# An attention and expert kernel on one Trainium2 core: the opening stage rebuilt, with folds of four head pairs side by side, five shared PSUM banks, stacks of eight heads moved one by one, and another order of steps

## What is computed

```
q = (xn @ q_a[h]) @ q_b[h];  k = (xn @ k_a[h]) @ k_b[h]     # 16 heads, 256 -> 64 -> 16
v = xn @ v_w.T + v_b
att = softmax(causal(q @ k.T / 4));  y = att @ v
out1 = y @ o_w.T + o_b
probs = softmax(xn @ choice_w.T)        # 8 experts, each takes its 128 best tokens of a batch
out2[tokens of e] += gate * (silu(xn[tokens] @ w1[e]) @ w2[e])
result = x + out1 + out2
```

## Time and profile before

| | us |
|---|---|
| median of three runs | 1244.37 (1242.15 to 1245.09) |
| the profiled execution | 1248.95 |
| its span, first to last instruction | 1247.2 |
| TensorE busy | 1163.1 (93%) |
| VectorE busy | 1013.3 (81%) |
| ScalarE busy | 682.7 (55%) |
| GpSimd busy | 702.6 (56%) |
| mean granted TensorE clock | 0.973 of full |

### The profile page before, as it was taken

One profiled execution on the slowest core, in us unless ns is written; L12 is line 12 of the kernel. 1 busy time (PEld: TensorE's weight loads), 2 busy tenths in 40 slices (PEclk: granted clock), 3 DMA queues, 4 the chain that ended last, 5 costly groups with the idle time before them and its releaser, 6 DMA issues. The chain is left out here.

```text
span 1247.2 us, 26009 instructions
## 1 busy us (share of the span) xinstructions
PE 1163.1 (93%) x8508; PEld 812.9 (65%) x8508; DVE 1013.3 (81%) x3396; ACT 682.7 (55%) x1330; POOL 702.6 (56%) x1021
## 2 busy tenths in 40 slices
PE   6789999999999999999999998869999999999994
PEld 5535556556556555555555554448989999999994
DVE  3589988988889999999999988679967676777762
ACT  2347777777677676676676666543423243333330
POOL 1235354354354354354354366754888888888875
PEclk9779999999999999999999999889999999999997
DMA  7552553553453552552551644224666666566654
GB/s 146 119 120 71 135 121 88 135 120 94 129 120 91 133 120 79 130 134 66 140 132 58 149 113 131 65 72 115 127 126 120 113 125 136 112 114 141 107 77 46
DMA packets 112730, 139.39 MB, mean 112 GB/s; under 512 B 21836, under 2 KB 79828, under 8 KB 112596
## 3 DMA queue, kind: packets, MB, share of 16 engines
q1 hardware_dynamic: 82756, 102.84, 32.3%
q0 software_dynamic: 24576, 33.57, 16.2%
q10 hardware_dynamic: 5264, 1.32, 0.6%
HBM read 53.22 MB, written 33.55 MB: 70 GB/s over the span
## 5 line engine op out<-in xcount | busy, mean ns | idle before, releaser
L808 DVE CUSTOM_DVE_ANT_0 junk<-bank,rowmask 128x256 bf16<-128x256 f32 (+3 forms) x1024 | 446.7, 482 | 48.9 <-PE bank L958 44.9
L660 ACT ACTIVATE probs<-bank 128x512 f32<-128x512 f32 x640 | 365.9, 596 | 134.1 <-PE bank L979 127.3
L560 POOL TENSOR_SCALAR_AFFINE_SELECT probs<-probs 128x256 f32<-128x256 f32 (+1 forms) x640 | 229.3, 372 | 255.7 <-ACT probs L660 252.4
L958 PE MATMUL bank<-kstk,qstk 96*128 96x256 bf16 (+3 forms) x1024 | 249.6, 305 | 14.0 <-DMA kstk<-qk_part 7.7
L979 PE MATMUL bank<-qstk,kstk 98*128 98x256 bf16 (+3 forms) x1024 | 250.0, 306 | 11.8 <-DMA qstk<-maxrow 9.7
L1142 POOL DMA_INDIRECT out_rows<-mixed,rows x128 | 212.1, 1657 | 58.3 <-issue 37.5
L1000 PE MATMUL bank<-probs,vaug 128*32 128x512 f32 (+3 forms) x2048 | 179.7, 446 | 5.0 <-POOL probs L560 5.0
L979 PEld LDWEIGHTS bank<-qstk,kstk 98*128 98x128 bf16 x1024 | 76.3, 98 | 148.3 <-ACT probs L660 91.7
L1166 ACT ACTIVATE hid<-bank 128x512 f32<-128x512 f32 x128 | 76.4, 598 | 172.3 <-PE bank L1259 146.6
L1277 PE MATMUL bank<-w_hi,hid_hi 128*128 128x256 f32 x512 | 147.3, 288 | 0.0
L1277 PE MATMUL bank<-w_hi,hid_lo 128*128 128x256 f32 x512 | 144.9, 283 | 0.0
(11 more groups left out here) (149 smaller groups left out, 2171.7 us busy)
## 6 DMA issues: line engine op xcount, KB each, us to landing
qstk<-qk_part SPq DMA_DIRECT2D x96, 256.0 KB, 5.1
kstk<-qk_part SPq DMA_DIRECT2D x96, 256.0 KB, 5.0
qstk<-in_L_ffn_w SPq DMA_DIRECT2D x32, 512.0 KB
xln<-in_L_attn_hidden_states SPq DMA_DIRECT2D x16, 512.0 KB, 6.7
xn_rows<-xn SPq DMA_DIRECT2D x16, 512.0 KB, 2.9
xres<-in_L_attn_hidden_states SPq DMA_DIRECT2D x16, 512.0 KB, 4.0
out_rows<-xres SPq DMA_DIRECT2D x16, 512.0 KB
out_rows<-mixed,rows POOLq DMA_INDIRECT x128
```

Source lines behind the costliest of these rows:

```text
L560: nc.gpsimd.affine_select(out=block, in_=block, compare_op=ALU.is_ge, fill=0.0, base=0, pattern=[[0, len(cols)], [1, P]], channel_multipli ...
L660: nc.scalar.activation(probs[n % 2][:, 512 * k:512 * k + 512], SCORET[k % 2][:], ACT.Exp, scale=SCALE).then_inc(exp_done, 1)
L808: last = nc.vector.tensor_tensor_reduce(out=junk[k % 2][:, col:col + width], in0=SCORE[score_bank(UN * n + k)][:, col:col + width], in1=ro ...
L958: last = nc.tensor.matmul(SCORE[score_bank(UN * n + k)][:, col:col + width], qstk[b % 2][0:KS, GH * g + h, P * i:P * i + P], kstk[b % 2][0 ...
```

## The change

It touches the opening stage, and with the stacks also every later batch:

- A fold is made in two steps. The new step `foldm` puts the second factor on the stationary side and the transposed first factor on the moving side (128 columns); four pairs of heads write to four strips of 32 partitions. Its result is copied out by ScalarE, and `fold` is now two 128x128 transposes. The columns come out so that a projection tile holds eight neighbouring heads.
- In the opening the shared steps take five banks in turn (two shared, two of `scoret`, one of the values' product); from the first `score` on, two in turn as before.
- Each projection tile is stacked as soon as it is ready: four times six DMAs per batch, of half the size. In batch 0 the six of k's first eight heads are issued by ScalarE's queue (new step `stack`), and the first scores wait for the first eight heads of q and of k alone.
- The loads are in another order (one of q_a first, then x, then the rest; the other weights are issued by ScalarE only ahead of `fold` 1), and so are the steps. The projections of batch 1 begin after eight units of scores instead of after one; the transposes of its xn stand among the scores.
- 42 transposes of the identity into a bank that nobody reads (`warm`).
- The bias products move behind the first scores.

```diff
-    out = [("xload", 0, 0), ("lnstat", 0, 0), ("lnstat", 0, 1), ("lnapply", 0, 0), ("xload", 1, 0)]
-
-    out += foldt(0) + [("fold", 0, 0)] + foldt(1) + [("xt", 0, 0), ("xt", 0, 1), ("fold", 1, 0)]
-    out += foldt(2) + qk(0, 0) + foldt(3) + qk(0, 1)
-    out += [("mid", 0, 0), ("fold", 2, 0), ("mid", 0, 1), ("fold", 3, 0), ("wv", 0, 0), ("wv", 1, 0)]
-    out += [("lnstat", 1, 0), ("lnstat", 1, 1)] + qk(0, 2) + qk(0, 3)
-    out += [("mid", 0, 2), ("v", 0, 0), ("mid", 0, 3), ("v", 0, 1), ("v", 0, 2), ("lnapply", 1, 0), ("v", 0, 3)]
-    out += [("xt", 1, dt) for dt in range(DT)] + [("wo", dt, 0) for dt in range(DT)] + [("ob", 0, 0)]
+    out = [("warm", 16, 0), ("xload", 0, 0)] + foldt(0) + [("lnstat", 0, 0), ("lnstat", 0, 1)]
+
+    out += [("foldm", 0, 0), ("fold", 0, 0), ("warm", 8, 0)] + foldt(1) + [("lnapply", 0, 0), ("xload", 1, 0), ("warm", 8, 0)]
+    out += foldt(2) + [("foldm", 1, 0), ("xt", 0, 0), ("xt", 0, 1), ("fold", 1, 0)] + foldt(3) + [("foldm", 2, 0), ("fold", 2, 0)]
+    out += [("qk_first", 0, 0), ("foldm", 3, 0), ("qk", 0, 0), ("fold", 3, 0), ("mid", 0, 0), ("qk_first", 0, 2), ("qk_first", 0, 1)]
+    out += [("qk", 0, 2), ("qk", 0, 1), ("mid", 0, 2)] + qk(0, 3) + [("wv", 0, 0), ("wv", 1, 0), ("warm", 10, 0)]
+    out += [("stack", 0, 2), ("mid", 0, 1), ("mid", 0, 3), ("lnstat", 1, 0), ("lnstat", 1, 1), ("v", 0, 0), ("v", 0, 1)]
+    out += [("wo", 0, 0), ("wo", 1, 0), ("v", 0, 2), ("v", 0, 3), ("lnapply", 1, 0)]
     for t in range(UN):
         out.append(("score", 0, t))
-        if t in (0, 2, 4, 6):
-            out += qk(1, t // 2)
-        if t in (2, 4, 6):
-            out.append(("mid", 1, t // 2 - 1))
+        out += {2: [("xt", 1, 0)], 4: [("xt", 1, 1)], 6: [("bias", 0, 0)], 7: qk(1, 0), 9: qk(1, 1)}.get(t, [])
     for t in range(UN):
-        out += [("score", 1, t)] + [("maxt", 0, 0)] * (t == 2) + [("maxd", 0, 0)] * (t == 3) + [("mid", 1, 3)] * (t == 4)
+        out += [("score", 1, t)] + [("maxt", 0, 0)] * (t == 2) + [("maxd", 0, 0)] * (t == 3)
+        out += {1: [("mid", 1, 0)] + qk(1, 2), 4: [("mid", 1, 1)] + qk(1, 3), 6: [("mid", 1, 2)], 8: [("mid", 1, 3)]}.get(t, [])
     for t in range(UN):
         out += [("scoret", 0, t), ("score", 2, t)] + [("maxt", 1, 0)] * (t == 3) + [("maxd", 1, 0)] * (t == 4)
+        out += [("ob", 0, 0)] * (t == 5)
...
+    for n, s in enumerate(shared):
+        bank_at[s] = n % 5 if n < len(opening) else n % 2
...
-            SCORE, SCORET, Y, SHARED = banks[0:3], banks[3:5], banks[5], banks[6:8]
+            SCORE, SCORET, Y, SHARED = banks[0:3], banks[3:5], banks[5], banks[6:8] + banks[3:6]
...
-                        elif kind == "mid" and k % 2 == 1:
-
-                            if n >= 2 and k == 1:
+                        elif kind == "mid":
+
+                            if n >= 2 and k == 0:
                                 sp.wait_ge(scoret_ready, at(UN * GB * (n - 1), 8 * UN))
                                 sp.sem_inc(sp_past, 1)
-                            sp.wait_ge(lo_done, at(GB * n + k + 1, 2 * GB))
-                            side = k // 2
+                            sp.wait_ge(lo_done, at(GB * n + turn(n, k) + 1, 2 * GB))
+                            side, m = divmod(k, 2)
                             stk = (qstk, kstk)[side][n % 2]
+                            landed = first_heads if n == 0 and m == 0 else stacked[n % 2]
+                            if n == 0 and k == 2:
+                                continue
                             for t, term in enumerate(TERMS):
-                                sp.dma_start(stk[t:KS:len(TERMS), :, :],
-                                             qk_part[term[side]][:, 2 * side:2 * side + 2, :]).then_inc(stacked[n % 2], 16)
+                                sp.dma_start(stk[t:KS:len(TERMS), H // 2 * m:H // 2 * m + H // 2, :],
+                                             qk_part[term[side]][:, k, :]).then_inc(landed, 16)
...
+                            if n == 1 and k == 0:
+                                act.wait_ge(first_heads, STACK_DMAS // 2)
                             if n >= 1 and k == 0:
-                                act.wait_ge(stacked[(n - 1) % 2], at(STACK_DMAS * ((n - 1) // 2 + 1), STACK_DMAS))
+                                act.wait_ge(stacked[(n - 1) % 2], landed_by(n - 1))
                             nc.scalar.activation(qk_part[0][:, k, :], src[:], ACT.Copy).then_inc(hi_done, 1)
...
-                        elif kind == "fold":
+                        elif kind == "foldm":
 
                             if n % DT == 0:
                                 pe.wait_ge(fold_b_in[n // DT], 16 * 2)
                             await_units(step, [("foldt", n, half) for half in range(2)], at)
                             for c in range(H // 2):
-                                last = nc.tensor.matmul(dst[:, 2 * HD * c:2 * HD * c + 2 * HD],
-                                                        fold_t[n][c // 4][:, P * (c % 4):P * (c % 4) + P],
-                                                        foldb[:, n // DT, c, :], start=True, stop=True)
+                                half, r = divmod(c, 4)
+                                last = nc.tensor.matmul(dst[2 * HD * r:2 * HD * r + 2 * HD, P * half:P * half + P],
+                                                        foldb[:, n // DT, c, :], fold_t[n][half][:, P * r:P * r + P],
+                                                        start=True, stop=True)
...
+                        elif kind == "warm":
+
+                            for _ in range(n):
+                                nc.tensor.transpose(banks[0][:, 0:P], ident[:], ident[:])
```

More of the change, by code:

```diff
@@ L228, in build @@
     assert len([s for s in every if s[0] == "moe"]) == len(set(s for s in every if s[0] == "moe"))
-    shared = [s for s in every if s[0] in ("foldt", "fold", "wv", "wo", "ob", "xt", "qk", "v", "maxt", "ytr", "yt", "o",
+    shared = [s for s in every if s[0] in ("foldt", "foldm", "fold", "wv", "wo", "ob", "xt", "qk", "v", "maxt", "ytr", "yt", "o",
                                             "rankt", "rowst")]
-    unit_of = {s: n for n, s in enumerate(shared)}
+    opening = [s for s in every[:every.index(("score", 0, 0))] if s in set(shared)]
+    bank_at, ordinal, filled_so_far = {}, {}, [0] * 5
+    for n, s in enumerate(shared):
+        bank_at[s] = n % 5 if n < len(opening) else n % 2
+        ordinal[s] = filled_so_far[bank_at[s]]
+        filled_so_far[bank_at[s]] += 1
     split_of = {s: n for n, s in enumerate(s for s in shared if s[0] in ("fold", "wv", "wo", "xt", "qk", "yt"))}
-    U_PAIR, S_PAIR = 48, 16
+    S_PAIR = 16
     x_v = x.rearrange("b (t p) d -> b p t d", p=P)
@@ L362, in build @@
             xn_stored = sem("xn_stored")
[L363 to L364 removed]
+            shared_ready = [sem(f"shared_ready{u}") for u in range(5)]
+            shared_done = [sem(f"shared_done{u}") for u in range(5)]
             hi_done = sem("hi_done")
@@ L869, in await_units @@
                 def await_units(step, sources, at):
-                    other = [s for s in sources if bank_of(s) != bank_of(step)] if step in unit_of else sources
-                    for u in range(2):
+                    other = [s for s in sources if bank_of(s) != bank_of(step)] if step in bank_at else sources
+                    for u in range(5):
                         mine = [s for s in other if bank_of(s) == u]
                         if mine:
-                            pe.wait_ge(shared_done[u], emptied(max(mine, key=unit_of.get), at))
+                            pe.wait_ge(shared_done[u], emptied(max(mine, key=ordinal.get), at))
                 def steps(todo, at):
```

109 lines of the change are left out of this document (72 added, 37 removed).

## The result

The changed kernel takes **1225.8 us** (median of 4, 1223.87 to 1229.86) against 1243.88 for the kernel before in the same comparison: 0.9865 of its time, 95% interval 0.9847 to 0.9882. That is 18.1 us less by the medians and 16.8 by the ratio, which compares the means of the executions other than the profiled ones; the forecast was 1228.4, the range 1220 to 1240. The profiled execution took 1225.27, its span is 1223.5. (Between the two profiled executions the difference is 23.7; the one of before lay 5 us above its median.)

The account below looks back on a forecast made before the run. Engines bound the steady stretch (TensorE busy 551 of 570 us, VectorE 529), so an earlier start ends earlier. Opening -16.0 and later batches 0 give 1232.95 against the profiled execution, 1228.4 us against the median; range 1220 to 1240.

Parts of the forecast that it names:

- Part 1: Opening loads: q_a's first half landed at 5.6 us instead of 7.76, the last factor at about 14 instead of 20.
- Part 2: Opening folds: 0.8 us less TensorE time for each of four; ScalarE's weight issues hold fold 1 for 2.6 us.
- Part 3: Opening, from the folds to the first score: at 34.7 us instead of 53.38, 18.7 earlier.
- Part 4: Opening, to VectorE's first row maximum: at 37.6 us, 16.5 earlier, behind ScalarE's issues, low parts and the normalisation.
- Part 5: First row maximum to first transposed score: 18.9 us, bound by VectorE, mark at 56.5; opening sum -16.0 us.
- Part 6: Every later batch, with twice the stack issues on SP: between -5 and +7 us, taken as 0.
- VectorE's statistics not waiting for x: Sign expected in the profile after: VectorE has no wait for the load of x.
- Clock low in the opening: Rival: TensorE's clock stays low in the opening despite the warm transposes; 1230 to 1240, named 1234 us, chance 0.18.
- x late: Rival: the load of x is late in every batch, 0.5 us x 13 = 6.5; 1235 us, chance 0.15.
- Half-size pieces at half the rate: Rival: stack DMAs move at 100 GB/s, 1.25 us each instead of 0.62; slower than before, 1267 us, chance 0.07.
- Whole stack binds: Rival: ScalarE's wait for batch 0's whole stack binds in the opening, 4 to 6 us given back; 1233 us, chance 0.1.
- the mark of 73.19: First transposed score before the change, forecast at 56.5 us; the prediction is wrong if it moves by less than 12.

Follow-up runs that it names:

- e11: The changed kernel itself, unedited, run and profiled again: 1224.34 us, ratio 0.9864 to the kernel before.
- e4: The changed kernel with the opening's loads in the old order, the other weights issued by ScalarE at the start: 1229.03 us, ratio 0.9896.
- e7: The changed kernel with the other five weights issued by SP behind the load of x 1, not by ScalarE: 1224.83 us, ratio 0.9857.
- e8: The changed kernel with the six DMAs of k's first stack issued by SP, not by ScalarE: 1223.09 us, ratio 0.9857.
- e1: The changed kernel without its 42 transposes of the identity: 1222.23 us, ratio 0.9822.
- e3: The changed kernel with its first score waiting for the stacks of all sixteen heads, not the first eight: 1232.44 us, ratio 0.991.
- e6: The changed kernel with each later batch's load of x issued ahead of k's stack: 1216.7 us, ratio 0.979.
- e12: The changed kernel without its 42 transposes of the identity, e1 again, run beside e11: 1221.35 us, ratio 0.982.
- e10: The changed kernel with the edits of e6, e7 and e8 together, and without the 42 transposes of the identity: 1210.08 us, ratio 0.9749.
- e13: The changed kernel with the edits of e6, e7 and e8 together, keeping the 42 transposes of the identity: 1212.61 us, ratio 0.975.
- e2: The changed kernel with two shared banks in the opening instead of five: 1232.25 us, ratio 0.9913.

## Why the prediction was right, and where it was off

**The mechanism held.** The opening moved the first transposed score by 14.2 us (15.4 in e11) where 16.7 were forecast, and the steady part gave little back or forth. The forecast of -16.0 came within 2.1 us of the measured -18.1, but by two errors that partly cancel, which is luck: the opening gained 1.3 to 2.5 less, the rest of the program 3 to 5 more (2.7 to 3.9 gained where 0.7 was to be given back). That gain was not foreseen and is not explained. By the traces it lies behind the twelve batches: from there to the end the kernel before took 535.8 us, the changed kernel 528.6 and 523.2, while the twelve took 566.2 against 563.8 and 568.8. There is one trace of the kernel before, from an execution 5 us above its median, so a part of this is that execution.

**Part 1, the loads.** q_a at 5.6: 5.24. But q_b was only called "as before", and no wait for it stood in the sum: TensorE waited 1.77 us for it, and `foldm` 0 began at 8.37. The order as a whole is worth 3.2 to 4.7 us (e4).

**Part 2, the fold.** TensorE's parts were near the forecast (0.85 and 0.3): eight products 0.64, two transposes 0.41. ScalarE's five issues were taken at 2.6 and took 3.05 (16.59 to 19.64), beginning 0.9 later; the high part of fold 1 came at 19.69 against 18.3. e7 shows what they hold up: without them on ScalarE that copy comes 1.9 us earlier.

**Part 3, the first score.** k's tile was complete at 26.7 (forecast 25.1), the low part at 30.0 (28.2). From there the DMAs went almost as forecast: the last was issued 3.3 us after the first (forecast 3.1) and landed 3.2 to 3.4 later (forecast 3.2), by 36.8. What failed is that the landing was taken as what the score waits for. The score stood behind v's matmuls, which waited 2.33 us for ScalarE's copies behind those issues, and came 0.6 later still. So the 2.7 us by which 37.4 misses 34.7 are 1.8 from parts 1 and 2, 0.3 from the DMAs and 0.6 from v.

**Part 4, the first row maximum.** The chain was named link by link and each is in the rows. Forecast 32.2 for the end of the issues, 34.6 came: 1.8 late at their start, and 4.51 instead of 3.9 for the six (3.92 to 5.11 in the other executions). From there to the maximum 5.4 were forecast and 5.6 measured. So 2.4 of the 2.6 us were there when the issues ended. e8 confirms the chain by removal.

**Part 5.** 18.9 forecast, 18.8 measured (59.02 less 40.23), but the agreement is luck: the same kernel took 16.8 in e11 (57.82 less 41.05). In the first profile the products of batch 1's first projection ran at half the clock (0.43 apart where full clock gives 0.24) and VectorE idled 1.14 us for them. Take the eight executions with five banks and no wait for the whole stack in this stretch. In four the clock was at half for 3.4 to 4.4 us of it, and it took 16.8 to 17.0 (e1, e3, e6, e11); in four for 7.9 to 10.1, and it took 18.0 to 18.8 (the first profile, e4, e7, e12). So the forecast was some 2 us too long at the higher clock. The first copy of batch 1 waited for TensorE, not for the stack, as forecast with 1 us of cover; e8 shows the wait when the cover is gone.

**Part 6, later batches.** Forecast 0, from -5 to +7. The loss was named: VectorE waited 6.5 us for x (8.1 in e11), and e6 shows that moving the load ahead gives 6.7 back. That the size agrees to the digit is luck, 7 waits of up to 1.8 where 13 of 0.5 were put, and the sign "VectorE's statistics not waiting for x" did not come. Nor has the landing of x, put at 4 us, a row: its median was 6.9 before and 4.9 after. The gain was put in the wrong place. "Gain at most the 4.9 us that TensorE waited for k's stack" failed: that wait grew to 6.9 (9.1 in e11), since k's second half is issued behind the first and x; in e6 it is 3.1. Other waits shrank: TensorE's for the maxima from 4.9 to 0.2 (0.8 in e11), VectorE's for scores from 22.8 to 15.5 (19.0). It fits that half-size DMAs clear the queues sooner, but no run isolates this, and the twelve batches are not measurably shorter than before.

**The rivals.** *Clock low in the opening*: it was low for part of 8 to 14 us and from 36 to 50. By the eight executions under part 5, some 4 to 7 us more at half clock go with 1 to 2 us in the last mark, not the six of the rival; this is a comparison of executions, and no run sets the clock. *x late*: true as a mechanism, 6.5 us, but it does not show in the length of the twelve batches against the kernel before. *Half-size pieces at half the rate*: refuted. 1 KB pieces move at 200 to 210 GB/s while a stack is under way, what the stacks with 2 KB pieces had the earlier trace rows, and a DMA lands in 2.5 us. The mean busy share of the DMA engines in the steady part fell from 0.46 to 0.40 for the same bytes. The Trainium skill's minimum of 2 KiB per partition ("DMA: Bandwidth & Descriptors", in the section on why a DMA increments its semaphore by 16), which is for 128 partitions, does not show in these copies of 16 partitions within SBUF; as the rate of issue sets their 205 GB/s, they don't test how fast 1 KB pieces could go. *Whole stack binds*: not here, but in e8, e10 and e13, where ScalarE waits 3.8 to 4.4 us for it. Of the two tests named beforehand, the mark of 73.19 moved by more than 12, and TensorE's waits for k's stack in the steady stretch did grow beyond 5 us. By that test the prediction called itself wrong, though the time came in its range: the test took one wait for the length of the batch.

**The working.** The bounds of the forecast, as listed, add up to 1222.4 to 1240.7 and not to 1221 to 1235. The rest of a split is counted as 0.62 us in part 5, where the earlier trace rows have 0.69. The terms of the landing add up to 34.5, given as 34.7. The result lies inside either range.

## What to carry to other kernels

An issue of these stack DMAs costs the engine that makes it some 0.65 us, as much as ScalarE's copy of 512 columns (0.60), for 128 KB and for 256 KB alike, and everything behind it in that engine's queue is late by the sum: ask for each issue who stands behind it, and give it to a queue where nobody does. When a transfer is cut in two, the issues double, so look at what else shares the queue: here one load of x, moved ahead of the split stack, gave 6.7 us beside the 18 of the whole change. In a serial opening look at the order of steps and the PSUM banks together: with two shared banks this order gave 6.5 to 8 us less than with five. And profile the same kernel twice before reading a mark to the microsecond.

## What the runs showed of the hardware

- Six issues of a stack take 3.8 to 4.1 us on SP's queue in the steady part, for 128 KB and for 256 KB each. In the opening k's first six took anything from 3.92 (e2) to 5.11 (e7) on ScalarE's queue and 3.83 (e10) to 4.71 (e13) on SP's; in the changed kernel the last of the six alone took 1.19. What decides between these is open.
- Whether TensorE's clock rises in the first 6 us differs between executions with identical instructions in front (1.09 to 1.97 us for the same eight transposes). In the changed kernel, e1 and e7 to e13, nine executions, it falls to half for some time between 36 and 50 us, each time behind idle time of TensorE; in the changed kernel it was busy 1.87 of 4 us from 32 to 36, in e7 1.08.
- Marks and medians agree only roughly. The first transposed score moved by 9.0 to 10.2, 3.8 to 2.6 and 1.9 to 0.7 us (e2, e8, e7, against the two profiles of the changed kernel), the medians by 6.5 to 8, 1.3 to 2.7 and -0.5 to 1.0.
